# Cross-attention in a two-layer decoder: one PSUM bank for the context in place of two, one more for the scores

## What is computed

```python
q_hk = (hidden_q @ Wq.T).reshape(b, s, H, K)
q_big = jnp.einsum('bshk,hkq->bshq', q_hk, w_kc_q)
...
kv_rope = kv_c * cos[None] + _rotate_half(kv_c) * sin[None]
q_r = jnp.einsum('bshq,hqr->bhsr', q_big, W_qr)
k_r = jnp.einsum('bld,hdr->bhlr', kv_rope, W_kr)
scores = jnp.einsum('bhsr,bhlr->bhsl', q_r, k_r)
attn = jax.nn.softmax(scores, axis=-1)
ctx_c = jnp.einsum('bhsl,bld->bhsd', attn, kv_rope)
ctx_lat = jnp.einsum('bhsd,hkd->bshk', ctx_c, w_kc_kv)
out = ctx_lat.reshape(b, s, H * K) @ Wo.T
```

## Time and profile before

| | us |
|---|---|
| median of 3 runs | 1490.22 |
| lowest and highest | 1486.14, 1491.39 |
| the profiled execution, its own time | 1497.55 |
| its span, first to last instruction | 1495.7 |

### The profile page before, as it was taken

One profiled execution on the slowest core, in us unless ns is written; L12 is line 12 of the kernel. 1 busy time (PEld: TensorE's weight loads), 2 busy tenths in 40 slices (PEclk: granted clock), 3 DMA queues, 4 the chain that ended last, 5 costly groups with the idle time before them and its releaser, 6 DMA issues.

```text
span 1495.7 us, 22043 instructions
## 1 busy us (share of the span) xinstructions
PE 1226.5 (82%) x7024; PEld 830.7 (56%) x7024; DVE 927.6 (62%) x2269; ACT 592.9 (40%) x1524; POOL 547.8 (37%) x629
## 2 busy tenths in 40 slices
PE   7688888999849877689999989999899705988981
PEld 3555554666624365457677346643566604777770
DVE  1678786643597975839955876668665442444443
ACT  2247776774531102558810146621665121222220
POOL 2244673542242413525510014410343163444444
PEclk9899999999979978889997999999999957999996
DMA  7275993000001001010030000000400442554544
GB/s 278 77 224 167 305 313 116 1 1 1 29 1 42 1 1 71 3 54 2 2 120 0 0 0 1 1 1 1 197 1 30 188 154 74 85 81 79 82 70 105
DMA packets 69615, 110.75 MB, mean 74 GB/s; under 512 B 5056, under 2 KB 59840, under 8 KB 66240
## 3 DMA queue, kind: packets, MB, share of 16 engines
q1 hardware_dynamic: 58896, 96.62, 19.1%
q0 software_dynamic: 10608, 12.72, 5.9%
HBM read 57.41 MB, written 51.91 MB: 73 GB/s over the span
## 4 chain that ended last, share of the span: by engine, by line
PE 60%; DVE 17%; issue 8%; ACT 6%; DMA 4%; POOL 3%; another core or an unknown queue 1%; SPq 1%; POOLq 0%; DVEq 0%; ACTq 0%
PE ps L692 8%; PE ps L681 7%; PE ps L967 6%; PE ps L701 4%; PE ps L673 3%; PE ps L674 3%; PE ps L1021 2%; DMA sums<-mem 2%; ACT mem L1664 2%; PE ps L1018 2%; PE ps L948 2%; PE ps L641 2%; PE ps L803 2%; DVE mem L1155 1%; PE ps L786 1%
## 5 line engine op out<-in xcount | busy, mean ns | idle before, releaser
L1858 POOL TENSOR_SCALAR mem<-mem 128x512 f32<-128x512 f32 x256 | 178.3, 698 | 414.2 <-DVE mem L1160 411.3
L1155 DVE TENSOR_REDUCE mem<-ps 128x1 f32<-128x512 f32 x256 | 176.0, 688 | 132.4 <-PE ps L674 124.2
L1656 ACT ACTIVATE mem<-ps,mem 128x512 f32<-128x512 f32 x256 | 177.1, 692 | 123.6 <-DVE mem L1155 122.3
L681 PE MATMUL ps<-mem 128*128 128x128 f32 x1024 | 157.4, 277 | 35.4 <-ACT mem L1664 30.4
L681 PEld LDWEIGHTS ps<-mem 128*128 128x128 f32 x1024 | 120.5, 141 | 95.1 <-POOL mem L1858 67.6
L1924 POOL DMA_INDIRECT sums<-mem x63 | 97.1, 1541 | 131.6 <-DVE mem L1532 98.6
L673 PE MATMUL ps<-rounded_at 128*128 128x512 f32 x256 | 124.3, 486 | 11.7 <-DVE rounded_at L1144 10.4
L692 PE MATMUL ps<-mem 128*64 128x256 f32 x1024 | 124.8, 386 | 2.4 <-ACT mem L1664 2.4
L1664 ACT ACTIVATE mem<-ps 128x512 f32<-128x512 f32 x192 | 114.4, 597 | 6.3 <-PE ps L681 5.9
L1868 POOL TENSOR_TENSOR mem<-mem 128x512 f32<-128x512 f32 x40 | 55.4, 1384 | 139.2 <-DVE mem L1196 139.1
L1638 ACT ACTIVATE rounded_at<-ps 64x512 fp32r<-64x512 f32 x64 | 37.8, 591 | 166.3 <-PE ps L950 154.2
(11 more groups left out here) (259 smaller groups left out, 2622.9 us busy)
## 6 DMA issues: line engine op xcount, KB each, us to landing
slots<-mem SPq DMA_DIRECT2D x15, 2312.0 KB, 10.0
mem<-in_f_w_dram SPq DMA_DIRECT2D x16, 1024.0 KB, 10.4
mem<-slots SPq DMA_DIRECT2D x63, 136.0 KB
mem<-in_f_w_dram SPq DMA_DIRECT2D x24, 256.0 KB, 3.4
mem<-in_x_wq_dram SPq DMA_DIRECT2D x2, 2048.0 KB, 13.2
mem<-in_x_wo_dram SPq DMA_DIRECT2D x2, 2048.0 KB, 8.5
mem<-sums SPq DMA_DIRECT2D x8, 256.0 KB, 4.5
mem<-in_x_wqr_dram SPq DMA_DIRECT2D x1, 1536.0 KB, 6.6
```

What stands on the lines that cost most here:

```text
L681: mm = pe.transpose(ps[3 + j % 2][:, k * P:(k + 1) * P], PR[j % 6][:, k * P:(k + 1) * P], ident)
L1155: dve.tensor_reduce(nmax[:, i % 8:i % 8 + 1], ps[SB[lay][i % len(SB[lay])]][:, :], AX.X, ALU.max, negate=True)\
L1656: act.activation(PR[i % 6], ps[SB[lay][i % len(SB[lay])]][:, :], ACT.Exp, bias=nmax[:, i % 8:i % 8 + 1], accum_out=esum[:, i % 8:i % 8 + 1 ...
L1858: pool.tensor_scalar(PR[i % 6], PR[i % 6], rinv[:, i % 8:i % 8 + 1], 1.0, ALU.mult, ALU.mult)\
```

## The change

The context product of every group goes to bank 5, and waits for the copy of the group just before. Bank 6 becomes a fourth bank of scores in layer 0 and a fifth in layer 1; the wait of the scores follows from the length of the list.

```diff
-        SB = [[1, 2, 7], [0, 1, 2, 7]]
+        SB = [[1, 2, 7, 6], [0, 1, 2, 7, 6]]
...
-                        if g >= 2:
-                            pe.wait_ge(x_ctx, g0 + g - 1)
+                        if g >= 1:
+                            pe.wait_ge(x_ctx, g0 + g)
                         for k in range(KC):
                             for hh in range(2):
-                                mm = pe.matmul(ps[5 + g % 2][64 * hh:64 * hh + 64, 0:S], KV[:, b * KC + k, 0, :],
+                                mm = pe.matmul(ps[5][64 * hh:64 * hh + 64, 0:S], KV[:, b * KC + k, 0, :],
...
-                        act.activation(CT[lay][:, p, b * S:(b + 1) * S], ps[5 + g % 2][:, 0:S], ACT.Copy).then_inc(x_ctx, 1)
+                        act.activation(CT[lay][:, p, b * S:(b + 1) * S], ps[5][:, 0:S], ACT.Copy).then_inc(x_ctx, 1)
```

## The result

| | before | changed |
|---|---|---|
| runs | 4, median 1489.33 us (1486.14 to 1491.39) | 4, median 1548.56 us (1539.57 to 1555.57) |
| profiled execution | 1497.55 us, span 1495.7 | 1546.92 us, span 1545.1 |
| granted clock, mean | 0.928 | 0.925 |

The ratio is 1.0377, 95% interval 1.0341 to 1.0414. The two medians of the table by themselves are 59.2 us apart, a ratio of 1.0398, which lies inside that interval. So by the ratios the change costs some 3.5 to 3.8%, 53 to 56 us. Of all the runs one, a run of e4_three_scores, took 1853.08 us at a granted clock of 0.637, and it counts in no ratio.

A forecast was written before the change was run, and what follows sets the result against it. TensorE was taken to bound cross-attention. Context-copy waits of 24.2, 1.3, 9.1, 16.2 and 0.5 us sum to 51.3, score banks and clock 0; added to the median 1490.2 that gives 1541.5 us, range 1531 to 1553, upper end stretched to 1562.

The forecast's parts named there:

- What bounds the group: Cross-attention: TensorE sets the pace with a few short waits per group of four units; VectorE and ScalarE start each group drained.
- The rival that the delay is absorbed: Context product is delayed but the group is not, since the next turn's wait does not move with it: 1490 us, chance 0.04.
- One sign of being right: TensorE's busy time unchanged, listed beside about 50 us of copy waits in 58 groups and layer 1's period at 7.15 to 7.25.
- The score banks, 0: Scores in both layers: one more bank gains nothing; bounds nothing and 1.3 us, taken as 0 because the POOL wait closes gaps.
- The rival that they held ScalarE back: Scores of steps 2, 3 and 0: one more bank lets ScalarE move ahead, 20.9 us go, 1469 us; chance 0.03.
- The context bank, 51.3 us in 58 groups: Context product waits for the previous group's ScalarE copy: 0.93 us per steady layer 1 group, 51.3 us in all.
- the upper end of 0.15: Lag from ScalarE's copy end to the context product: 0.11 us taken, 0.15 as upper end, which adds 2.3 us.
- Which 58: Groups with the new wait, in both layers; one just behind the queries of layer 0's second half was to wait for nothing new.
- The last but one product of layer 0: Context product near the end of layer 0: new wait of 0.17 us, with 0.28 for the last.
- The clock, 0: TensorE's granted clock stays at 1.00 despite the new waits, about 1.3 us idle per 7.17 us group in layer 1; cost 0.
- The priced fall of 1.7 us: Rival, clock falls too: 1.7 us per fall, 1570 us with 17 falls, 1640 with 58; chance 0.09.
- main range: Main case's own range, 1531 to 1553 us: score waits, lag, profile gaps and run spread around 1541.5; new wait alone, chance 0.84.

The follow-up runs named there:

- e4_three_scores: Three score banks in place of four in layer 1, two context banks kept, against the kernel before: 1492.44 us, ratio 1.0012.
- e1_wait_alone: Changed kernel with the score banks of the kernel before, one context bank kept, bank 6 unused in cross-attention: 1548.63 us, ratio 1.0386 to the kernel before.
- e6_layer1_only: The change made in layer 1 alone, against the kernel before: 1510.89 us, ratio 1.0151.
- e5_late_copy: Changed kernel with ScalarE's context copy one step later, at the end of step i%4==1: 1637.5 us, ratio 1.1013 to the kernel before.
- e9_late_copy_filled: Late-copy kernel plus six idle-filling matmuls before each waiting context product of layer 0, score banks as before the change: 1597.51 us, ratio 1.0748 to the kernel before.
- the second set: Six more runs of the changed kernel, unaltered: 1542.03 us, ratio 1.0353 to the kernel before.

## Why the prediction was right

The forecast was 1541.5 us, 51.3 us more than before; measured were 1548.56 and, again, 1542.03. The mechanism was the one forecast. That the terms agree to a few tenths of a microsecond is in part luck, as two of the points below show.

- **What bounds the group.** Right: the waits are the ones named, and VectorE and ScalarE are drained at each start. After the change they are idle for 1 us longer and nothing else moves. The rival that the delay is absorbed fell with the period of 7.22 us. One sign of being right did not come as written: TensorE's busy time over the span rose from 1226.5 to 1235.7 us. In cross-attention it nearly stayed (211.4 and 211.7 us in layer 0, 254.2 and 255.9 in layer 1); the rest lies in stretches that were not changed.
- **The score banks, 0.** Right in sum (e1_wait_alone, e4_three_scores) and in its working: the gain at the start of layer 0 is taken back at the turn behind it, which starts 5.14 us after the first scores in both traces. The rival that they held ScalarE back fell with both runs.
- **The context bank, 51.3 us in 58 groups.** The trace has 51.4 us in 58 waits. In layer 1 the wait is 0.90 where 0.93 was forecast, but TensorE's period grew by 0.98: the column of idle time leaves out what the engine's modelled ends overlap, so the two are not quite the same thing. The lag from the copy to the product was 0.14 us here, near the upper end of 0.15, not 0.11. With 0.14 the term is 53.0, and the two layers have grown by 52.7. The 51.4 us also hold 0.79 that were there before: the last product of layer 0 now waits 1.11 us for the context copy, where it had waited 0.79 for its probabilities. That is 0.32 more, where 0.28 was forecast.
- **Which 58.** One of them was another group than forecast. The product behind the queries of layer 0's second half waits 1.11 us where 0 was expected. In the kernel before, the granted clock had fallen there (0.66 in the five microseconds from 245), the turns ahead of the product were slow, and the copy was ready in time; in the changed kernel the clock stayed at 1.00 there, TensorE came earlier and waited. The distance from product to product over that place did not grow (25.74 us before, 25.48 after), but only because the one trace of the kernel before had that fall in it. In e6_layer1_only, with the same layer 0 and a clock of 1.00 there, the distance is 24.31 us. Against that the new wait costs 1.2 us, a term that the forecast put at nothing. The last but one product of layer 0 shows no wait, where 0.17 was expected.
- **The clock, 0.** Right for the change, and the doubt was well placed. In the steady stretches waits near 1 us left it alone; waits of 1.95 to 2.64 us in layer 0 mostly did not, and cost 40 us there (e5_late_copy, e9_late_copy_filled). The priced fall of 1.7 us was of the right size: 39.3 us over the 23 groups with a slow product is 1.7 us each. The rule of the Trainium skill ("TensorE: Matmul & The Clock Gate", section "A second HAM failure mode: psum-queue depth-cycling") was not borne out in the changed kernel, which cycles banks with about 1.3 us of waits a group at a clock of 1.00. With the later copy the clock did swing in layer 0, as the rule has it. That section gives no count of falls; one in each group was the prediction's own reading.
- **The rest.** The median of the first runs lies 7 us above the forecast; the second set lies 0.5 us above. What stands between them is spread in the runs, whose place was not looked for. The parts that the prediction names for its main range come to 1532 to 1552, not 1531 to 1553; both medians lie inside either.

## What to carry to other kernels

A bank is held from the first write to the copy that empties it, and that copy's place in its engine's queue decides for how long. Before adding a bank, see whether the matmul itself ever waits for one (not its weight load, whose 20.9 to 23.2 us of idle time cost nothing here); before taking one away, see how long after the product its copy stands in the queue, and whether it can be moved into a hole of that engine. The bank freed in this way was worth some 24 us as a third bank of turned probabilities, where a wait for a bank lay on the path, and nothing as one more bank of scores.

## What was not expected of the hardware

How little separates a clock of 1.00 from one that falls. With TensorE idle for 1.57 us in one piece per group of 7.9 us (layer 1 of e5_late_copy) the granted clock was 1.00. In layer 0 of the same kernel, with 1.95 to 2.64 us, it was 0.81 and 0.89 on average over two stretches, while five groups in a row kept the full level at 1.95 us. The falls cost some 40 us beside the waits. Six matmuls per group of layer 0 that compute nothing brought the clock back to 1.00 and those 40 us with it.
